# Selective scan and routed experts: C rows on ScalarE's queue, eight tap loads a tile, another order in the first two routing tiles

## The reference, cut to what matters

```python
def step(state, xs):                       # scan over 1024 tokens, 4 batches, 1024 channels, 16 states
    d_t, B_t, C_t, u_t = xs
    dA = jnp.exp(d_t[..., None] * A)
    state = state * dA + (d_t * u_t)[..., None] * B_t[:, None, :]
    y_t = jnp.einsum('bdn,bn->bd', state, C_t)
    return (state, y_t)
...
x = x + jnp.tanh(g_xattn[0]) * scan_block(ctx, layernorm(x))
# second block, h = layernorm(x), 4096 tokens of 1024 channels
scores = jax.nn.sigmoid(h @ gate_w.T)      # 32 experts, best 2 of 4 groups, then best 4
out = moe(h, topk_idx, topk_w, w1, w2, w3) # at most 256 tokens per expert, order of arrival
shared = jax.nn.silu(h @ shared_gate) * (h @ shared_up) @ shared_down
x = x + jnp.tanh(g_ffn[0]) * (out + shared)
```

## Time and profile before

| what | us |
|---|---|
| median of three runs | 3978.18 |
| lowest, highest | 3975.20, 3978.39 |
| the profiled execution | 3982.52 |
| its span on the core | 3980.7 |
| GpSimd busy in L1125 (512 units of the scan) | 1205.6 |
| VectorE busy in L1108 (512 scans) | 1134.9 |
| ScalarE busy in L1078 and L1070 | 583.5 + 547.2 |
| idle before L1125 | 29.0 |

### The profile page before, as it was taken

The page is one execution under the profiler, slowest core; times in us unless marked ns, Lnnn a source line. Parts: engine busy times, 40 slices in busy tenths (PEclk is TensorE's granted clock), DMA queues, the critical chain, the costliest instruction groups (busy, mean ns, idle before and its releaser), DMA issues. The chain is left out here.

```text
span 3980.7 us, 58840 instructions
## 1 busy us (share of the span) xinstructions
PE 3674.5 (92%) x20528; PEld 3047.7 (77%) x20528; DVE 3058.8 (77%) x3680; ACT 2147.4 (54%) x2642; POOL 1931.1 (49%) x1169
## 2 busy tenths in 40 slices
PE   8898488888888888869999989999999999999998
PEld 3444388878878888858888868888888888888887
DVE  7898899999999999988888756666666666455555
ACT  3687689989989989942222234444444444200000
POOL 0233099999999999932222243333333333222221
PEclk9999599999999999989999989999999999999999
DMA  7677853563463473367777657777777777677543
GB/s 238 233 288 275 292 163 120 142 178 117 130 189 112 120 211 101 113 208 247 243 238 244 240 192 252 252 252 250 249 252 252 252 253 250 236 279 257 194 161 122
DMA packets 374393, 835.44 MB, mean 210 GB/s; under 512 B 96656, under 2 KB 155792, under 8 KB 364880
## 3 DMA queue, kind: packets, MB, share of 16 engines
q1 hardware_dynamic: 339264, 765.97, 56.8%
q0 software_dynamic: 34816, 67.24, 5.8%
q10 hardware_dynamic: 144, 0.00, 0.0%
HBM read 619.21 MB, written 245.27 MB: 217 GB/s over the span
## 5 line engine op out<-in xcount | busy, mean ns | idle before, releaser
L1125 POOL TENSOR_TENSOR h<-h,c 128x1024 f32<-128x1024 f32 x512 | 1205.6, 2411 | 29.0 <-DVE h L1108 25.9
L1108 DVE TENSOR_TENSOR_SCAN h<-da,dbu 128x1024 f32<-128x1024 f32 x512 | 1134.9, 2272 | 50.7 <-ACT dbu L1070 28.4
L1157 PE MATMUL psy<-ident,h 128*128 128x128 f32 x4096 | 562.2, 281 | 82.6 <-POOL h L1125 61.2
L1078 ACT ACTIVATE da<-dl,ad 128x1024 f32<-128x1024 f32 x512 | 583.5, 1140 | 101.8 <-DVE h L1108 89.9
L1906 POOL DMA_INDIRECT xg<-scratch_xn,ids x256 | 328.6, 1284 | 592.6 <-DVE xT_place L2199 511.6
L1070 ACT ACTIVATE dbu<-psb 128x512 f32<-128x512 f32 x1020 | 547.2, 588 | 35.0 <-PE psb L1147 34.1
L1157 PEld LDWEIGHTS psy<-ident,h 128*128 128x128 f32 x4096 | 444.6, 142 | 131.4 <-POOL h L1125 92.8
L2204 DVE TENSOR_TENSOR wsp<-arena,wsp 128x2048 fp32r<-128x2048 f32 x146 | 329.6, 2285 | 91.8 <-ACT wsp L2149 91.8
L1443 POOL DMA_INDIRECT scratch_tab<-tok_s,si_s x128 | 125.4, 980 | 459.4 <-DVE si_s L1822 375.7
L1147 PE MATMUL psb<-m,du_taps 128*128 128x128 f32 x2048 | 292.8, 290 | 42.4 <-ACT dbu L1070 35.8
L1147 PEld LDWEIGHTS psb<-m,du_taps 128*128 128x128 f32 x2048 | 257.6, 192 | 78.9 <-ACT dbu L1070 73.7
(11 more groups left out here) (246 smaller groups left out, 8544.8 us busy)
## 6 DMA issues: line engine op xcount, KB each, us to landing
arena<-in_w SPq DMA_DIRECT2D x192, 1024.0 KB, 6.7
du_taps<-scratch_duT SPq DMA_DIRECT2D x496, 128.0 KB, 2.9
c<-scratch_c SPq DMA_DIRECT2D x64, 512.0 KB, 13.1
scratch_xT<-xT_s SPq DMA_DIRECT2D x32, 1024.0 KB
scratch_ob<-ob SPq DMA_DIRECT2D x64, 512.0 KB, 2.6
xT_place<-scratch_xT SPq DMA_DIRECT2D x32, 1024.0 KB, 4.9
scratch_duT<-duT SPq DMA_DIRECT2D x52, 512.0 KB, 4.1
xz<-in_x SPq DMA_DIRECT2D x32, 512.0 KB, 5.5
```

The source lines that it names most:

```text
L1078: act.activation(da[k % 2][:, :], dl[:, i % 2, :], ACT.Exp, scale=ad[:, i % 2, n:n + 1]).then_inc(s_da, 1)
L1108: dve.tensor_tensor_scan(h[:, k % HR, :], da[k % 2][:, :], dbu[:, (k // GN) % 2, k % GN, :], 0.0, ALU.mult, ALU.add).then_inc(s_scan, 1)
L1125: pool.tensor_tensor(h[:, k % HR, :], h[:, k % HR, :], c[:, n, :], ALU.mult).then_inc(s_hc, 1)
L1157: mm = pe.matmul(psy[:, t, :], h[:, k % HR, t * P:(t + 1) * P], ident[:], is_transpose=True, start=(n == 0 and t % 4 == 0), stop=(n == NST ...
```

## The change

Three parts, all in the two functions above.

1. C rows of batches 1 to 3 leave SP's queue. ScalarE issues row n itself, behind the copies of unit k, for the unit `USED` = 5 before it, and waits for GpSimd's count of that unit. The rows of batch 0 stay on SP.
2. A part of the taps is loaded with two loads of 64 partitions (256 KB) instead of four of 32 partitions (128 KB), so eight instead of sixteen a tile; TensorE waits for half the count.
3. In the first two tiles of routing, the split of the down weights (`weight_head(2)`, `weight_rest(2)`) moves behind the first normalisations of tile 2; `multiply(0)` and `first_rest(1)` move ahead of `choose(0)`; the queue positions of tile 0 move on TensorE behind the logits of tile 1; `multiply` waits also for the logits' Tanh.

```diff
             def load_du / SP:
                 for part in range(2):
-                    for twin in range(2):
-                        sp.dma_start(f32(duT[part * 2 * TB + twin:(part + 1) * 2 * TB:2, r * CP:(r + 1) * CP, :]),
-                                     dr["duT"][i, twin][:, r * CP:(r + 1) * CP, :]).then_inc(s_du[r], 16)
+                    sp.dma_start(f32(duT[part * 2 * TB:(part + 1) * 2 * TB, r * CP:(r + 1) * CP, :]),
+                                 dr["duT"][i][:, :, r * CP:(r + 1) * CP, :].rearrange("w t c e -> t w (c e)")).then_inc(s_du[r], 16)
...
-            def load_c(b, n):
-                after(sp, s_hc, (b * ET - 1) * NST + n + 1 if b else 0)
-                sp.dma_start(c[:, n], dr["c"][b, n].partition_broadcast(P)).then_inc(s_cl[n], 16)
+            def load_c(n):
+                sp.dma_start(c[:, n], dr["c"][0, n].partition_broadcast(P)).then_inc(s_cl[n], 16)
...
+            def next_c(used):
+                b = used // (ET * NST) + 1
+                if used >= 0 and used // NST % ET == ET - 1 and b < B:
+                    n = used % NST
+                    act.wait_ge(s_hc, used + 1)
+                    act.dma_start(c[:, n], dr["c"][b, n].partition_broadcast(P)).then_inc(s_cl[n], 16)
...
                 copy_input(k + AHEAD)
+                next_c(k - USED)
...
-                        pe.wait_ge(s_du[r], i * 64)
+                        pe.wait_ge(s_du[r], i * 32)
...
             TensorE, routing:
                         h_transpose(t - 1)
+                    if route and second and not first:
+                        positions(t - 1, True)
...
-                    if route and not last:
+                    if route and not last and not first:
                         positions(t, first)
...
             ScalarE, routing:
                         normalise(1, 0, 1)
+                        weight_head(2)
                         normalise(2, 1, 0)
...
                 gate_tanh()
-                weight_head(2)
...
             VectorE, routing:
                 dve.wait_ge(s_u, t + 1)
+                if route:
+                    dve.wait_ge(s_th, t + 1)
...
+                    if route and first:
+                        multiply(t)
+                        first_rest(1)
                     if route:
                         choose(t)
...
                     if route and first:
-                        multiply(t)
-                        first_rest(1)
                         norm(2, 1, 0)
+                        weight_rest(2)
...
                 dve.tensor_scalar(gate2[:], gate[:], SCALE, None, ALU.mult)
-                weight_rest(2)
```

More of the change, by code:

```diff
@@ L903, in selective_scan @@
         GATED_AT = 8
+        USED = 5
         FIRST = 5
@@ L1017, in _ @@
             for n in range(FIRST):
-                load_c(0, n)
+                load_c(n)
             load_u(0)
@@ L1026, in _ @@
                 turn = i % ET == ET - 1 and b < B
-                turned = i % ET == 0 and i
                 final = i == NU - 1
@@ L1030, in _ @@
                     load_delta(i + 1)
-                if turned:
-                    for n in range(10, 12):
-                        load_c(b, n)
                 if i:
@@ L1036, in _ @@
                     load_u(i)
-                if turned:
-                    for n in range(12, NST):
-                        load_c(b, n)
                 if turn:
                     load_m(b, 0)
-                    for n in range(4):
-                        load_c(b, n)
                 for r in range(PARTS):
@@ L1052, in _ @@
                     load_m(b, 1)
-                    for n in range(4, 10):
-                        load_c(b, n)
             store(NU - 1)
```

## The result

The changed kernel takes 3999.89 us (median, 3997.7 to 4000.9), the kernel before 3976.69 beside it on the same chip. The ratio is 1.0057 with a 95% interval of 1.0044 to 1.0070: **23 us slower**, where 17 us of gain were forecast. It lies outside the range.

The account below looks back on a forecast made before the run. GpSimd was taken to bound the scan, TensorE routing from tile 2 on. Waits at the turns -17.2, gate tile +3 x 0.8, routing -2.3 gave -17.1 us: 3978.2 to 3961 us, range 3955 to 3974.

Parts of the forecast that it names:

- The bound, and what a turn holds: Scan: GpSimd sets the pace; 17.2 of its 29.0 us idle lie at the three ends of a batch.
- The remark that there is no idle time at the other 28 tile borders: Scan: GpSimd's idle time stands at the turns of the batch alone, with none at the other 28 tile borders.
- The step that failed: Scan turns: taps, no longer behind C rows, issue and land in 4.2 to 9.3 us, hidden under 9.4 us of units.
- the 17.2 us then go in full: Scan turns: moving C rows and enlarging tap loads removes all 17.2 us of GpSimd's waits.
- the sum: Whole kernel: -17.2 us of waits, +3 x 0.8 for the gate tile, -2.3 for routing, giving -17.1 us.
- The second rival: Scan turns: taps still land late because loads share the DMA engines; half the stall stays, 3968.5 us, chance 0.13.
- ScalarE's issue: Scan turns: 48 C-row issues on ScalarE, bounded from nothing to 4.8 us a turn, taken at 0.8 for the gate tile.
- The first and third rival: The first: ScalarE pays for its issues in full, 14.4 us at the turns, 3973 us, chance 0.17. The third rival follows.
- The third rival: Scan turns: ScalarE held by a full queue once eight rows pile up, six expected at most; 3996 us, chance 0.09.
- The second tap wait: First tile of a new batch: TensorE's 2.79 us wait for taps at 834.42 goes, no tap wait above 1 us.
- Part 3: the mechanism: Routing: an 8 us TensorE wait moves the clock's fall to tile 0's down product; tile 3 starts 2.3 us earlier.
- The lower end of the prediction's bound: ScalarE at a turn: the 0.43 us issue runs during the second copy (0.588 us) and costs nothing.

Follow-up runs that it names:

- `e17_before_half`: Kernel before, C rows of batches 1 to 3 loaded by half, order and queue unchanged (half the C values left out): 3961.52 us against 3974.06, ratio 0.9966.
- `e6_sp_times`: Kernel before, with C rows 4 to 7 put ahead of and between the four parts of the taps on SP's own queue: 3998.73 us, ratio 1.0053.
- `e8_small_m`: Changed kernel, matrix loads of batches 1 to 3 cut from 2048 to 64 elements a row (most B values left out): 3983.97 us, ratio 1.0018.
- `e12_half_rows`: Changed kernel, C rows of batches 1 to 3 loaded by half (half the C values left out): 3973.27 us against 3976.10, ratio 0.9990.
- `e9_order`: Kernel before, on SP's queue C rows 0 to 3 moved behind the last tile's taps, rows 12 to 15 ahead of the next u load: 4001.27 us, ratio 1.0062.
- `e3_routing`: Kernel before with only the new order of the first two routing tiles: 3976.29 us, ratio 1.0001.
- `e5_hold`: Changed kernel, ScalarE issuing only C rows 0 to 3 in a batch's last tile and rows 4 to 15 in the new batch: 3989.91 us against 3976.83, ratio 1.0030.
- `e16_early_two`: Kernel before, with C rows 0 and 1 moved on SP's queue between the store and the u load of the last tile: 3976.96 us against 3974.06, ratio 1.0002.

## Why the prediction was wrong

**The bound, and what a turn holds: right.** GpSimd's waits at the turns were the place (17.2 us), and `e17_before_half` gives them back: 29.0 - 12.1 = 16.9 us of idle time less, 12.5 by the medians. The remark that there is no idle time at the other 28 tile borders was a little too strong: the earlier trace rows itself has 0.83 us at one of them.

**The step that failed: "At a turn the taps are no longer behind C rows. I take 1.3 + 2.9 to 1.3 + 8 = 4.2 to 9.3 us for issue and landing: all of it is under 9.4."** The landing alone took 12.0 us for the first half of the loads and 15.3 for the second (medians). The upper end of 8 us came from loads that stand behind four C rows already in the queue. That is a price for a backlog that is worked off once, in order. In the changed kernel the rows aren't ahead of the taps in a queue, but new ones are asked for every 2.4 us while the taps are under way, and they take 60% of the DMA engines. SP's queue in the old order gave the taps a protection that I read as a hindrance: rows 4 to 9 stood behind them. `e6_sp_times`, which gives this up on the same queue, has the whole loss. The sentence on the earlier trace rows looked only at what stands ahead in the queue, and not at what would newly be asked for beside it: eight rows from 771.7 to 787.8 us, before the last taps are issued, while before only rows 0 to 3 were asked for until the taps were out. So of "the 17.2 us then go in full" nothing came; 17.7 us were added.

**What the sum had no term for.** The reading of a turn named one wait of TensorE, 2.79 us for the taps. The trace of before also has 1.78 us for the taps of the last tile and 2.19 for u at the same turn. Neither these nor the second half of the matrix, waited for until 818.90 in the changed kernel and not at all before, has a term in the prediction.

**The full stretch was not looked at as a whole.** Before, the share of the engines is 0.91 to 1.09 in every window of 4 us from 772 to 816 us (two of these windows are in the earlier trace rows); bytes asked for earlier within it push others back. `e8_small_m` and `e12_half_rows` show that bytes taken out give time back: against the changed kernel's +23 us they stand at +7 and -3, and `e9_order` that bytes moved later come back as a later wait.

**The second rival had the right place and the wrong floor.** It said that "the taps still land late, since all loads share the DMA engines", and priced it by half of the stall. What is shared can get later than now; its price should have run past the stall of before to a loss. The Trainium skill, DMA: Bandwidth & Descriptors, section "Issuing engines are not separate DMA queues", says that loads of different engines interleave on the same DMA engines and a second issuer saves only issue time: the 60.4% and 40.2% of the two queues agree, and so does `e6_sp_times`. The section "Queues, rings and completion order" of the same page has each DMA engine take turns between the queues it has work for; that both queues moved data in the same 12 us fits this, but no run here shows the turns themselves, and the packets moved were not equal (485 and 293).

**ScalarE's issue: right, it costs nothing.** The first and third rival fell. The 48 issues take 0.326 to 0.355 us and run beside the copies:

```profile
787.67 0.60 ACT L1058 ACTIVATE dbu<-psb 128x512 f32<-128x512 f32 x1
787.82 0.33 ACTq L1068 DMA_DIRECT2D c<-scratch_c  x1
788.14 0.60 ACT L1058 ACTIVATE dbu<-psb 128x512 f32<-128x512 f32 x1
788.78 1.12 ACT L1074 ACTIVATE da<-dl,ad 128x1024 f32<-128x1024 f32 x1
```

The third rival's time (3996) is near the measured one by accident: its mechanism isn't in the trace. Its condition nearly came, though. The rows take 7.2 to 18.6 us to land, with one asked for in about 2.4, so by my estimate some seven are under way at once, more than the six that the prediction allowed, and no issue on ScalarE is held.

**The second tap wait: right.** The wait at 834.42 is gone, with taps landing after 3.5 to 4.6 us. The load of u is issued 9.5 us later at the first turn; TensorE waits less for it there (1.22 us, before 2.19), since TensorE is late itself, and more at the other two (2.4 and 2.6, before 1.0 and 1.2).

**Part 3: the mechanism right, its worth too small to be seen in the time.** The long wait ahead of the first down product came as forecast, 9.06 us against 8, the clock's fall was paid by this product (0.63 us a matmul, then 0.39), and the last wait shrank from 3.15 us to 0.96:

```profile
1800.65 0.76 PE L1492 MATMUL psO_s<-wsp_wide,hT_s 128*128 128x512 f32 x1 [9.06 <-DVE hT_s L1719]
1801.21 0.63 PE L1493 MATMUL psO_s<-wsp_wide,hT_s 128*128 128x512 f32 x1
...
1805.65 0.39 PE L1492 MATMUL psO_s<-wsp_wide,hT_s 128*128 128x512 f32 x1
...
1809.55 0.36 PE L1492 MATMUL psU_s<-wsp_wide,xT_s 128*128 128x272 f32 x1 [0.96 <-DVE sg_s L1726]
```

Tile 3 starts 83.2 us after GpSimd's last product (1827.07 and 1743.90 us), where before it was 85.8 (1811.39 and 1725.62): 2.6 us nearer, forecast was 2.3. A wait of 2.37 us at 1777.75 was not foreseen; the clock falls there too (0.43 us a matmul of 272 columns, 0.29 at the higher level). `e3_routing` by itself reads 1.0001 (0.9991 to 1.0010), so neither 2.3 us of gain nor zero is excluded.

**Open:** how much of the 26 us between whole and half rows at the new place (+23 and -3 against before) is the sum of bytes and how much their mixing with the taps; what the second queue costs by itself (`e5_hold`, and the 9.7 us at equal bytes); what the slow clock costs; and the first turn of `e16_early_two`.

## What to carry to other kernels

Before you take a load out of a queue because others wait behind it, look whether the DMA engines are full in the stretch and list what each load would newly run beside. In this kernel, where they are full, the order of SP's queue kept six rows behind the taps, and giving it up cost 22 us on either queue; neither earlier issue nor any other order that was tried won time. Name every load that is waited for in the stretch, and not only the longest wait. Price a shared resource past its present stall, to the side of a loss.

## What was not expected of the hardware

A DMA issue on ScalarE takes less than on SP (0.33 us against 0.43 for a C row) and hides in the copies around it, 48 times. The lower end of the prediction's bound had only assumed that.

The rate at a full share depends strongly on the mix: it is 409 GB/s where C rows are moved almost alone and 217 a few us earlier. The same loads can also take more or less of the DMA engines' time by their order: the 18.90 MB of the first turn took 73.9% of the engines' time from 764 to 848 us in `e9_order`, 82.0% in the kernel before and 86.4% in the changed one. The kernel with the least of it was not the fastest.
